# Rotations of the narrow attentions in two pieces, the second behind the next step's maxima

## The reference

```python
# self: 8 key heads, causal                 # cross: 32 key heads, keys from ctx
q = rope(x @ Wq); k = rope(x @ Wk)          q = axial_rope(x @ Wq, pos)
scores = q @ k.T                            k = axial_rope(ctx @ Wk, pos)
attn = softmax(scores / 4) @ (x @ Wv)       attn = softmax(q @ k.T / 4) @ (ctx @ Wv)
# rope: concat(x1*cos - x2*sin, x2*cos + x1*sin)
```

## Time and profile before

| | |
|---|---|
| median of 3 runs | 3669.28 us (3666.15 to 3674.68) |
| the profiled execution's own time | 3672.33 us |
| its span, first to last instruction | 3670.5 us |
| mean granted TensorE clock | 0.94 |
| busy: TensorE, VectorE, ScalarE, GpSimd | 3299.7, 2050.8, 1330.1, 569.7 us |
| narrow attentions | 1919.9 to 2941.5 us |
| their share of TensorE and VectorE busy time | 900.8 and 635.3 us |

### The profile page before, as it was taken

One profiled execution on the slowest core, in us unless ns is written; L12 is line 12 of the kernel. 1 busy time (PEld: TensorE's weight loads), 2 busy tenths in 40 slices (PEclk: granted clock), 3 DMA queues, 4 the chain that ended last, 5 costly groups with the idle time before them and its releaser, 6 DMA issues. The chain is left out here.

```text
span 3670.5 us, 54520 instructions
## 1 busy us (share of the span) xinstructions
PE 3299.7 (90%) x19769; PEld 2526.3 (69%) x19770; DVE 2050.8 (56%) x4964; ACT 1330.1 (36%) x2944; POOL 569.7 (16%) x621
## 2 busy tenths in 40 slices
PE   6999999999999999977958899889898857999995
PEld 6888888888888788843425565555455435787784
DVE  3555655566666666651155666666666645443445
ACT  0444434443444344431113343435444442122110
POOL 1333322222222222033141111210000000000000
PEclk7999999999999999988978999989999978999998
DMA  5111111111011011034340000000000011000001
GB/s 190 53 53 53 53 53 30 35 35 30 30 35 35 27 33 30 1 117 163 130 140 2 2 3 2 28 2 22 5 5 5 2 46 24 24 11 11 23 11 46
DMA packets 110615, 146.79 MB, mean 40 GB/s; under 512 B 23712, under 2 KB 72864, under 8 KB 109288
## 3 DMA queue, kind: packets, MB, share of 16 engines
q1 hardware_dynamic: 95904, 110.80, 9.4%
q0 software_dynamic: 14480, 32.91, 2.9%
HBM read 100.55 MB, written 42.08 MB: 39 GB/s over the span
## 5 line engine op out<-in xcount | busy, mean ns | idle before, releaser
L554 ACT ACTIVATE probs_w<-probs_w,low_w 128x256 f32<-128x256 f32 (+1 forms) x512 | 242.9, 475 | 589.7 <-DVE low_w L599 589.7
L1871 DVE TENSOR_REDUCE mx_n<-bank 128x6 f32<-128x768 f32 (+1 forms) x256 | 279.7, 1093 | 151.0 <-PE bank L1648 83.0
L1779 ACT ACTIVATE probsT_n<-bank 128x768 f32<-128x768 f32 (+1 forms) x256 | 235.8, 921 | 277.0 <-PE bank L1660 276.8
L572 DVE TENSOR_TENSOR probsT_lo_w<-bank,probsT_hi_w 128x384 fp32r<-128x384 f32 (+1 forms) x256 | 159.7, 624 | 125.7 <-ACT probsT_hi_w L537 124.9
L518 PE MATMUL bank<-wo_hi_w,oT_hi_w 128*128 128x512 f32 x512 | 211.4, 413 | 2.1 <-issue 2.1
L1642 PE MATMUL bank<-kT_n,qT_n 48*128 48x256 f32 (+1 forms) x1024 | 124.0, 322 | 94.2 <-DVE mx_n L1871 91.5
L518 PE MATMUL bank<-wo_hi_w,oT_lo_w 128*128 128x512 f32 x512 | 204.4, 399 | 0.0
L518 PE MATMUL bank<-wo_lo_w,oT_hi_w 128*128 128x512 f32 x512 | 204.4, 399 | 0.0
L582 DVE TENSOR_SCALAR probs_w<-probs_w,inv_w 128x256 f32<-128x256 f32 (+1 forms) x512 | 187.6, 408 | 20.8 <-issue 0.9
L2309 DVE SCALAR_TENSOR_TENSOR h<-bank,scale_now,silu 128x512 f32<-128x512 f32 x64 | 48.0, 750 | 202.5 <-PE bank L2202 202.5
L450 PE MATMUL bank<-xT_lo_w,wq_hi_w 128*128 128x512 f32 x512 | 161.1, 396 | 0.0
(11 more groups left out here) (362 smaller groups left out, 8141.3 us busy)
## 6 DMA issues: line engine op xcount, KB each, us to landing
expert_rows<-ctxT_hi_w SPq DMA_DIRECT2D x20, 512.0 KB, 4.3
work_m<-expert_rows SPq DMA_DIRECT2D x40, 256.0 KB, 2.6
expert_products<-work_m POOLq DMA_DIRECT2D x40, 256.0 KB, 2.7
staging_w<-in_L_attn_Wq SPq DMA_DIRECT2D x32, 256.0 KB, 3.0
expert_table<-ctxT_hi_w SPq DMA_DIRECT2D x16, 512.0 KB, 5.5
staging_w<-in_L_attn_Wo SPq DMA_DIRECT2D x32, 256.0 KB, 2.6
staging_w<-in_L_xattn_Wq SPq DMA_DIRECT2D x32, 256.0 KB, 2.6
staging_w<-in_L_xattn_Wo SPq DMA_DIRECT2D x32, 256.0 KB, 2.6
```

The costliest lines, as they stand in the source:

```text
L554: last = act.activation(pr, pr, ACT.Exp, bias=low[:, n % ROUNDS_OF_PROBS, tile:tile + 1], scale=-1.0, accum_out=den[:, n % ROUNDS_OF_PROBS ...
L572: return dve.tensor_tensor(dst, src, hi.bitcast(FP32), ALU.subtract)
L1779: act.activation(probsT[:, turn_ % SLOT_PAIRS, :, 0:cols], scoreT[:, :, 0:cols], ACT.Exp, scale=SCALE)\
L1871: dve.tensor_reduce(to.rearrange("p t h -> p h t"), seen, AX.X, ALU.max).then_inc(s["scores_read"], 1)
```

## The change

`rotate` ends where the PSUM bank is released. The rest, the SBUF half, becomes a function `divide`. For the tiles prepared ahead of the loop it follows at once. In the loop a rotated tile is remembered in `turned`; in the next step its `divide` is called behind the maxima of that step (the first integer of the early list) and ahead of all other work of the step; where a step has no maxima it is called first. So, on VectorE:

- q0 (step 0, late): SBUF half behind the maxima of pair 9 and the negation of group B, ahead of h1 and h3 in step 1;
- q1 (step 3): behind the maxima of pair 12, ahead of out0 in step 4;
- k0 (step 12): behind the maxima of pair 5 and the negation of group A, ahead of k1's PSUM half in step 13;
- k1 (step 13): behind the maxima of pair 6 in step 14.

`divide` begins with the drain that stood there. No other engine's program changes.

```diff
--- before.py
+++ after.py
@@ -1836,6 +1836,13 @@
                                  (slice(8 * i, 8 * i + 8), slice(8 - 8 * i, 16 - 8 * i)))
                     last = dve.tensor_tensor(u[:, :, to], b[:, :, other], wide(sin[:, to], 8), ALU.mult)
                 last.then_inc(s["prep_dve"], 1)
+
+            def divide(name, n):
+
+                t = int(name[1])
+                q = name[0] == "q"
+                heads_ = NH if q else kv_heads(n)
+                r, u = (a[:, 0:heads_ * HW].rearrange("p (h w) -> p h w", w=HW) for a in (rot, turn))
                 dve.drain()
                 dve.tensor_tensor(r, r, u, ALU.add)
                 dve.drain()
@@ -1951,15 +1958,28 @@
             dve.drain().then_inc(s["consts_ready"], 1)
             for name, n in before:
                 do(name, n)
+                if name in ("k0", "k1"):
+                    divide(name, n)
+            turned = None
             for n in range(-1, ITEMS):
                 for at in range(PAIRS):
                     early, late = step(n, at)
-                    for name, item in early:
+                    due, turned = turned, None
+                    for name, item in early + [(None, n)]:
+                        if due and not isinstance(name, int):
+                            divide(*due)
+                            due = None
+                        if name is None:
+                            break
                         do(name, item)
+                        if name in ("k0", "k1", "q0", "q1"):
+                            turned = name, item
                     if n >= 1 and at in (7, 8, 9, 10):
                         norm_stage(at - 7, n - 1)
                     for name, item in late:
                         do(name, item)
+                        if name in ("k0", "k1", "q0", "q1"):
+                            turned = name, item
             for name, n in after:
                 do(name, n)
             for part in range(4):
```

## The result

The changed kernel takes 3663.82 us (median of 20 runs, 3658.96 to 3670.59), the kernel before 3671.41 us (median of 20 runs on the same chips). The ratio is 0.9977, 95% interval 0.9970 to 0.9985: 7.6 us faster, about half of the 14 us forecast. The profiled execution has a span of 3668.0 us beside 3670.5.

What follows compares the result with a forecast made beforehand. TensorE, held by late maxima, was taken to bound the kernel; A -14, B -5, C +10 and D -5 sum to -14 us, from the profiled 3672.3 to 3658.3, or 3655 us as median, range 3633 to 3670.

Steps and rivals of the forecast that it cites:

- The rule: For each moved place: first maxima earlier by the SBUF half, second unchanged; gain depends on whether TensorE was already late there.
- A: Keys of cross items, 8 places (steps 12 to 14 of items 6 to 13): -14 us, between -19.5 and -7.
- B: Queries of cross items with cross heads behind, 6 places (steps 0 to 3, items 9 to 14): -5 us.
- C: Queries made during items 1 to 8, 8 places: no direct gain, slow clock on q1's projection, +10 us.
- An equal slow stretch: Self-item queries: lower-clock time of unchanged length moves 3.5 us, onto q1's projection, a loss of about 1.8 us each.
- The same work in another order ends at the same time: Self-item queries: VectorE has no gap until M(10) ends, so the wait reappears before S(11); direct gain nothing.
- the clock comes back as early as now: Low bound for the 8 query places of items 1 to 8: loss 0 each, against 2.3 us at the upper bound.
- D: First item and the step before it, where VectorE has slack behind q0 and q1: -5 us, bounds -8 and -2.
- At nothing: Keys of self items (7 places) and q1's rotation in later items: 0 us, TensorE being covered by its own work.
- My own signs: Expected in the changed kernel: cross items 63 to 65 us, self items 58 to 60; wrong if cross-item clock falls as often.
- The rival of a wait that only moves: Every early maxima is paid back at the next, A and B yield low ends: -3 us, 3666 us, chance 0.22.

## Why the prediction was right, and where it wasn't
**The rule was right.** "The first maxima comes earlier by the SBUF half, the second comes when it came before": S(10) and S(11) of the self item show it to within 0.6 us, and the run with q0 two steps later confirms it from the other side. There the maxima behind the moved piece has slack (M(11), beside q1's projection), and q0's piece is worth 61 us.

**A** is right in mechanism and, in the trace of the change, in size (-14.6 for -14). S(6) waits no longer, S(7) waits 1.4 us (1.7 forecast), S(8) comes 4.0 to 4.4 us after S(7) (3.65 with the clock up, 5.2 with it down). Alone it is worth 22 us, with an interval of 15 to 30. The middle of the two ends was 13.3, taken as 14.

**B** failed in the trace of the change (+1.2 for -5; alone it is not decided), in the step "S(11) then starts at 2663.2, 1.7 us earlier ... I take -5". In item 12, that of the earlier trace rows, S(11) comes 8.85 us after L1833 of q0 instead of 10.15, so 1.3 us earlier; over the six places it is 5.8 us in place of the 10 us. The head transposes wait 1.74 us for the normalisations and then run at the lower clock (2.03 us) in five of the six, so TensorE is late at S(11). Only in item 10, where they run at the full clock, does S(11) come when forecast (8.46 us after L1833). The second term is the lower clock on q1's projection. Its price, "about 1.5 us each", was near (1.7 us where it is new), but I put it in full only into the low end, as if it might not come. It came in all six places, where before it was in two: 5.48 us instead of 3.70 in item 12, but 5.59 and 5.54 in item 14, together 6.5 us more. Putting the heads first removed their wait and put one for M(10) in its place.

**C** failed in size: +10 forecast, +0.8 in the trace, 0.9993 alone. The wait moved as said (3.75 us before S(11)). Two terms were wrong. "An equal slow stretch": it is 3.4 us in place of 6.8 in five of the eight places, and 6.8 in three. In the item shown q1's projection costs 1.1 us more (5.29 for 4.20), over the eight places 7.2 us. And "The same work in another order ends at the same time": from L1833 to S(11) it is 8.45 us instead of 9.05, over the eight places 3.4 us less. The three instructions of the second piece take 2.35 us there in place of 2.72, since GpSimd's mask falls on them otherwise, and M(9) begins without the drain that stood between the two halves. The low bound, "the clock comes back as early as now", was nearer.

**D** held: -7.3 in the trace, -5.0 us alone by medians, for -5.

**At nothing** held the real miss: "Keys of self items (7 places): ... TensorE is covered by its own transposes". Those transposes are the ones that read the low parts. I had used M(6) and M(7) for the cost and not asked when each key's `split` is due: late in step 14 for k0, in step 15 for k1, one step behind the piece's new place. The transposes now wait (0.80 and 0.63 us), and the clock falls behind them in half of the places. It costs 13 us alone. How much of that is the waits and how much the clock is open; the run with k0 alone also moves M(6) and does not part them.

**My own signs.** Of the signs that I named, one came up that calls the prediction wrong: the clock falls in cross items about as often as before (at its lower level for 65 us from q0 of item 8 to q0 of item 15, 68 before). Self items take 59 to 62 us where I said 58 to 60, and no waits for maxima stand before S(8).

So the total came within the range partly by luck: two misses cancelled, 0 for +12 in the self keys against +10 for +1 in the self queries. B's miss of 6 us did not cancel. The rival of a wait that only moves (3666 us) stands closer to the median of 3663.8 than the forecast of 3655, but for another reason than it gave, since A did not yield its low end. What stays open: why the parts measured alone multiply to 0.991 and together give 0.9946, if that gap is real. The slow stretches of the clock lie differently in each trace (clock 0.50 in three of six like self items, not in the others), which fits, but no run isolates it.

## What to carry to other kernels
A piece of work moved past an urgent instruction lands in front of the next urgent one. It is gained only where that next one has slack, so look for the step in which the other engine has a long instruction of its own, and put it there: one step later the queries of items 2 to 9 were worth nothing, two steps later q0 of all items was worth 61 us. Before moving, list for the moved piece who reads its result and when, not only whom it delayed. And look what else the engine that is freed has to wait for: with k1 alone the gain at one wait went into the next, for a DMA. And when a change has several places, measure the places alone: this one held a gain of 22 us and a loss of 13.

## What the runs showed of the hardware
Where a wait of TensorE is placed matters beyond its length. With q0 two steps later a self item keeps clock 1.00 and falls from 58.0 to 53.8 us, 1.0 us more than the 3.25 us by which S(11) came earlier. With the change as it was, TensorE's waits for maxima fell by 33 us between 2000 and 2870 us and others rose by 20, but over the stage the projections of queries went from 650 to 710 ns a matmul.

VectorE's SBUF instructions and GpSimd's mask hold each other up in these traces. The add of 128x512 (L1840, L1847) takes 0.69 us alone and 1.02 us where it meets the mask, as in the item of the earlier trace rows:

```profile
2146.43 0.64 POOL L1546 TENSOR_SCALAR_AFFINE_SELECT probsT_n<-probsT_n 128x512 f32<-128x512 f32 x1 [6.07 <-ACT probsT_n L1779]
...
2146.59 1.02 DVE L1840 TENSOR_TENSOR rot_n<-rot_n,turn_n 128x512 f32<-128x512 f32 x1
```

In the changed kernel the mask takes 1.19 us instead of 0.64 where it began together with the add at 2151.31, and the cast behind the add 0.97 us instead of 0.69:

```profile
2151.31 1.19 POOL L1546 TENSOR_SCALAR_AFFINE_SELECT probsT_n<-probsT_n 128x512 f32<-128x512 f32 x1 [1.22 <-ACT probsT_n L1779]
```

The casts of the self keys (L1855, L1862) went from a mean of 291 to 375 ns, since some of them meet the mask in their new place. The Trainium skill ("SBUF — State Buffer", section "SBUF: two separate sides") describes it: VectorE and GpSimd share a port pair. GpSimd, or a VectorE instruction with two SBUF inputs or in a two-port mode, holds it for the whole instruction if it starts first, while the other is blocked. The rows agree in kind: each partner, in turn, lasts longer by 0.3 to 0.55 us. That the other is blocked in full they do not show: in the first two of these rows the mask had 0.48 us left when the add began, and the add took 0.33 us longer.
